# W_o's product in whole fp32 instead of three products of rounded parts, and new orders of work on all engines

## The reference

```
xn  = layernorm(x)                                       # plain
x2  = layernorm(xn) * ln_w + ln_b                        # the attention's own
q, k, v = x2 W_q + b_q, x2 W_k + b_k, x2 W_v + b_v       # 16 heads of 64
P   = softmax(q k^T / 8, causal)                         # 256 x 256 for each head
z   = P v                                                # per head
attn = sum over heads of z W_o + b_o                     # back to 128 features
Wq  = clip(round(W / (mean|W| + 1e-5)), -1, 1)           # ternary, for W1 and W2
ffn = relu(xn Wq1^T + b1) Wq2^T + b2                     # 512 hidden
out = x + attn + ffn
```

## Time and profile before

| | |
|---|---|
| runs | 227.25, 227.69, 225.07 us |
| the profiled execution | 226.65 us, its span 224.9 us |
| PE busy | 212.5 us (95%), 3670 matmul records |
| DVE busy | 202.1 us (90%) |
| ACT busy | 195.7 us (87%) |
| POOL busy | 182.5 us (81%) |
| granted TensorE clock | full (1.00) in all stretches |

### The profile page before, as it was taken

How to read it: one execution, slowest core, us unless ns; L and a number is a source line. 1 busy time by engine, 2 the same in 40 slices (tenths; PEclk the granted TensorE clock), 3 DMA queues, 4 the chain that set the end, 5 groups by cost and what they waited for, 6 DMA issues and landing times.

```text
span 224.9 us, 9676 instructions
## 1 busy us (share of the span) xinstructions
PE 212.5 (95%) x3670; PEld 187.4 (83%) x3670; DVE 202.1 (90%) x776; ACT 195.7 (87%) x733; POOL 182.5 (81%) x363
## 2 busy tenths in 40 slices
PE   7999799999999999989998999999997999999885
PEld 5666489779997999879997999989986998799674
DVE  3298999999999998999999999999999998899921
ACT  1799999989999889997999889997999799997740
POOL 5569999999979995899959995999959995955630
PEclk9999999999999999999999999999999999999999
DMA  5890538503875658624855658634865748638700
GB/s 149 273 281 6 124 72 219 155 0 59 236 190 136 138 109 208 146 54 111 184 153 136 127 112 217 137 67 111 188 154 126 142 102 207 166 66 210 167 11 23
DMA packets 24030, 30.79 MB, mean 137 GB/s; under 512 B 2608, under 2 KB 23088, under 8 KB 23984
## 3 DMA queue, kind: packets, MB, share of 16 engines
q1 hardware_dynamic: 23840, 30.16, 56.0%
q10 hardware_dynamic: 144, 0.02, 0.0%
HBM read 4.73 MB, written 1.05 MB: 26 GB/s over the span
## 4 chain that ended last, share of the span: by engine, by line
PE 38%; DVE 23%; DMA 11%; ACT 10%; POOL 8%; SPq 4%; issue 3%; POOLq 0%; DVEq 0%
DMA pT<-blocks 11%; DVE s_ps L604 9%; PE m_ps L863 6%; PE s_ps L823 6%; DVE blocks L617 6%; SPq L352 4%; ACT prob L492 3%; PE m_ps L941 3%; ACT prob L494 2%; PE m_ps L788 2%; PE s_ps L734 2%; DVE neg_max L604 2%; PE m_ps L790 2%; PE m_ps L789 2%; DVE zT_lo L623 2%
## 5 line engine op out<-in xcount | busy, mean ns | idle before, releaser
L492 ACT ACTIVATE prob<-s_ps,neg_max 128x256 f32<-128x256 f32 x128 | 65.4, 511 | 2.6 <-DVE neg_max L604 2.3
L315 POOL TENSOR_SCALAR prob<-prob,inv_sum 128x128 f32<-128x128 f32 x126 | 47.1, 374 | 22.1 <-DVE inv_sum L611 21.9
L604 DVE CUSTOM_DVE_ANT_0 s_ps<-s_ps,causal 128x256 f32<-128x256 f32 x128 | 55.8, 436 | 6.8 <-PE s_ps L823 6.5
L316 POOL TENSOR_SCALAR prob<-prob,inv_sum 128x256 f32<-128x256 f32 x126 | 61.3, 486 | 0.0
L617 DVE STREAM_TRANSPOSE blocks<-prob 128x768 f32<-128x768 f32 x62 | 58.8, 960 | 0.7 <-POOL prob L316 0.6
L863 PE MATMUL m_ps<-pT,v 64*64 64x64 f32 (+2 forms) x1536 | 50.0, 257 | 5.9 <-DMA pT<-blocks 3.5
L863 PEld LDWEIGHTS m_ps<-pT,v 64*64 64x64 f32 x1536 | 42.8, 133 | 12.1 <-issue 5.8
L494 ACT ACTIVATE prob<-s_ps,neg_max 128x128 f32<-128x128 f32 x128 | 51.7, 404 | 0.0
L823 PE MATMUL s_ps<-qk 64*64 64x128 f32 (+2 forms) x1280 | 49.7, 275 | 0.8 <-ACT prob L494 0.6
L823 PEld LDWEIGHTS s_ps<-qk 64*64 64x64 f32 x1280 | 42.1, 133 | 5.6 <-issue 3.3
L604 DVE CUSTOM_DVE_ANT_0 s_ps<-s_ps,causal_first 128x128 f32<-128x128 f32 x128 | 42.4, 331 | 0.0
(11 more groups left out here) (120 smaller groups left out, 492.1 us busy)
## 6 DMA issues: line engine op xcount, KB each, us to landing
pT<-blocks SPq DMA_DIRECT2D x124, 192.0 KB, 3.6
xT_cur<-in_xT SPq DMA_DIRECT2D x8, 128.0 KB, 4.6
outT<-out_sb SPq DMA_DIRECT2D x8, 128.0 KB, 4.1
x_all<-in_x SPq DMA_DIRECT2D x1, 768.0 KB, 8.9
wv_raw<-in_w_v SPq DMA_DIRECT2D x2, 256.0 KB, 5.9
wo<-in_w_o SPq DMA_DIRECT2D x1, 512.0 KB, 7.0
x_all<-in_x SPq DMA_DIRECT2D x2, 128.0 KB, 4.1
wq_raw<-in_w_q SPq DMA_DIRECT2D x2, 128.0 KB, 2.4
```

The lines of the kernel that those rows point to most:

```text
L315: op(first, first, inv_sum[:, j, 2 + h:3 + h], 0.0, ALU.mult, ALU.add)
L316: last = op(later, later, inv_sum[:, j, h:h + 1], 0.0, ALU.mult, ALU.add)
L492: nc.scalar.activation(later, s_ps[:, pair % 2, h, 0:S].rearrange("p (g j k) -> p g j k", g=TILES, j=QT), ACT.Exp, bias=neg_max[:, j, h:h ...
L604: last = nc.vector.tensor_tensor_reduce(out=sc, in0=sc, in1=mask, scale=-SCALE, scalar=-MASKED, op0=ALU.add, op1=ALU.min, accum_out=neg_ma ...
```

## The change: W_o and z stay whole, and the orders are new

W_o is kept as it comes from memory and z as one fp32 tile `zT`; each triple of float32r matmuls is now a single whole fp32 matmul. The two splitting steps of W_o and DVE's four `z` steps per batch are gone, with the tiles and semaphores that served them; where PE waited for DVE (`z_lo`) it now waits for ACT (`z_done`). P v itself (line 863) is as it was. All orders are written anew.

```diff
-PE_PLAN = ("s0 x0-:1 y0-:2 s1 z0- pr4:0 pr5:3 x1-:1 y1-:2 s2 z1- v0:0 pr6:3 x2-:2 y2-:1 s3 z2- s4 pr7:3 v1:0 "
-           "x3-:2 y3-:1 s5 z3- s6 v2:3 v3:0 xh+:2 oa-:1 f0:0 f1:2 s7 pr0+:0 xn+:3 pr1+:2 ob- pr2+:0 pr3+:3")
+PE_PLAN = ("pr5:3 x1-:1 y1-:2 s2 z1- s3 pr6:0 v0:3 x2-:1 y2-:2 s4 z2- pr7:3 x3-:1 v1:0 y3-:2 s5 z3- s6 v2:3 v3:2 "
+           "xh+:0 oa-:1 f0:0 f1:2 xn+:3 s7 pr0+:0 pr1+:2 ob- pr2+:3 pr3+:0 x0:2 s0+ y0:1 s1+ z0 pr4+:0")
...
-ACT_PLAN = ("e13- e14- pr0 xn e15- pr1 pr2 pr3 e0 z0- e1 e2 pr4 pr5 z1- e3 e4 e5 pr6 z2- e6 e7 e8 e9 pr7 z3- e10 "
-            "xh+ e11 e12 f0 f1")
+ACT_PLAN = ("e1 z0- e2 e3 pr4 pr5 z1- e4 e5 pr6 e6 z2- e7 e8 e9 pr7 z3- e10 xh+ e11 e12 e13 f0 xn+ f1 pr0+ pr1+ "
+            "e14 e15 pr2+ pr3+ e0+")
...
-DVE_PLAN = ("ln+ m2 z0- m3 i0 t7- m4 m5 z1- t0 i1 v0 m6 m7 z2- m8 m9 t1 i2 v1 m10 m11 i3 z3- v2 m12 i4 v3 xh+ t2 "
-            "t3 i5 m13 m14 m15 i6 t4 t5 xn+ t6 o- i7 m0+ m1+")
+DVE_PLAN = ("m2 m3 ln+ t7- i0 i1 m4 m5 t0 m6 v0 m7 t1 m8 i2 i3 m9 v1 m10 m11 i4 v2 m12 v3 xh+ m13 t2 t3 i5 xn+ i6 "
+            "t4 t5 m14 m15 t6 o- i7 m0+ m1+")
...
-POOL_PLAN = ("p1 ln+ p2 p3 xl+ p4 p5 p6 h0 p7 p0+ h1")
+POOL_PLAN = ("h0- h1- p0 p1 ln+ p2 p3 p4 xl+ p5 p6 p7")
...
-SP_PLAN = ("d3- d0 d1 d2 st-")
+SP_PLAN = ("d0 d1 d2 d3 st-")
...
-                nc.scalar.activation(zT_hi[:, 2 * duo:2 * duo + 2, :], heads_banks(duo, b), ACT.Copy).then_inc(z_hi, 1)
+                nc.scalar.activation(zT[:, 2 * duo:2 * duo + 2, :], heads_banks(duo, b), ACT.Copy).then_inc(z_done, 1)
...
-            def low_heads(b, duo):
-                wait(dve, z_hi, PAIRS // 2 * b + duo + 1)
-                both = slice(2 * duo, 2 * duo + 2)
-                nc.vector.tensor_tensor(zT_lo[:, both, :], heads_banks(duo, b), zT_hi[:, both, :].bitcast(F32),
-                                        ALU.subtract).then_inc(z_lo, 1)
...
                 for p in range(PAIRS // 2):
-                    nc.tensor.matmul(dst, wo_lo[:, p, :], zT_hi[:, p, :], start=False, stop=False)
-                    nc.tensor.matmul(dst, wo_hi[:, p, :], zT_lo[:, p, :], start=False, stop=False)
-                    nc.tensor.matmul(dst, wo_hi[:, p, :], zT_hi[:, p, :], start=False, stop=False)
+                    nc.tensor.matmul(dst, wo[:, p, :], zT[:, p, :], start=False, stop=False)
...
                     if p % 2 == 0:
-                        wait(pe, z_lo, DUOS * b + p // 2 + 1)
-                    nc.tensor.matmul(dst, wo_lo[:, p, :], zT_hi[:, p, :], start=False, stop=False)
-                    nc.tensor.matmul(dst, wo_hi[:, p, :], zT_lo[:, p, :], start=False, stop=False)
-                    last = nc.tensor.matmul(dst, wo_hi[:, p, :], zT_hi[:, p, :], start=False, stop=(p == PAIRS - 1))
+                        wait(pe, z_done, DUOS * b + p // 2 + 1)
+                    last = nc.tensor.matmul(dst, wo[:, p, :], zT[:, p, :], start=False, stop=(p == PAIRS - 1))
```

More of the change, by code:

```diff
@@ L58 @@
-ACT_HEAD = ("wh0 wh1 pr0 wh2 xn pr1 wh3 e0 e1 pr2 aa e2 pr3 e3 pr4 pr5 e4 e5 pr6 pr7 f0 e6 e7 xh+ e8 e9 xn+ f1 "
-            "e10 e11 pr0+ e12 e13 e14 e15 pr1+ oh z0 pr2+ e0+ wh4 e1+ pr3+ pr4+ z1 e2+ pr5+ e3+ e4+ e5+ z2 e6+ "
-            "wh5 e7+ pr6+ z3 e8+ e9+ xh++ pr7+ e10+ e11+ e12+ f0+ f1+")
-ACT_PLAN = ("e13- e14- pr0 xn e15- pr1 pr2 pr3 e0 z0- e1 e2 pr4 pr5 z1- e3 e4 e5 pr6 z2- e6 e7 e8 e9 pr7 z3- e10 "
-            "xh+ e11 e12 f0 f1")
-ACT_TAIL = ("e13- pr0 xn e14- pr1 e15- pr2 pr3 e0 e1 pr4 z0- e2 e3 z1- e4 e5 z2- pr5 e6 e7 pr6 e8 e9 pr7 z3- e10 "
-            "e11 e12 e13 z0 e14 e15 f0 z1 w6 w7 f1 z2 z3")
@@ L75 @@
-POOL_PLAN = ("p1 ln+ p2 p3 xl+ p4 p5 p6 h0 p7 p0+ h1")
-POOL_TAIL = ("p1 p2 p3 p4 p5 p6 h0 h1")
-SP_HEAD = ("d0 d1 d2 d3 d0+ d1+ d2+ st")
-SP_PLAN = ("d3- d0 d1 d2 st-")
-SP_TAIL = ("d3- d0 d1 d2 st- st")
+PE_HEAD = ("xb:1 pr0:3 pr1:1 xn:0 s0 pr2:3 v0:0 v1:2 s1 s2 v2:2 pr3:1 ta:0 pr4:3 s3 pr5:2 pr6:3 s4 v3:2 pr7:0 s5 "
[3 rows of a table added]
+PE_PLAN = ("pr5:3 x1-:1 y1-:2 s2 z1- s3 pr6:0 v0:3 x2-:1 y2-:2 s4 z2- pr7:3 x3-:1 v1:0 y3-:2 s5 z3- s6 v2:3 v3:2 "
+           "xh+:0 oa-:1 f0:0 f1:2 xn+:3 s7 pr0+:0 pr1+:2 ob- pr2+:3 pr3+:0 x0:2 s0+ y0:1 s1+ z0 pr4+:0")
@@ new lines @@
+PE_TAIL = ("s2 x1-:1 y1-:2 pr5:3 z1- s3 v0:0 pr6:2 pr7:1 v1:0 s4 x2-:2 y2-:3 s5 x3-:1 y3-:0 z2- z3- s6 v2:2 "
+           "oa-:3 x0:0 f0:2 y0:1 s7 ob- z0 x1:2 y1:3 f1:0 tw6:1 z1 v3:0 tn3:2 tw7:3 x2:0 y2:1 x3:3 y3:2 z2 z3 "
+           "oa:0 ob oc")
+ACT_HEAD = ("wh0 wh1 pr0 wh2 xn pr1 wh3 e0 e1 pr2 aa e2 e3 pr3 wh4 pr4 e4 e5 pr5 e6 e7 pr6 e8 e9 xh+ wh5 pr7 e10 "
+            "e11 f0 e12 pr0+ e13 pr1+ e14 e15 z0 e0+ pr2+ xn+ f1 e1+ pr3+ pr4+ pr5+ e2+ e3+ z1 e4+ e5+ e6+ pr6+ "
+            "e7+ z2 e8+ e9+ pr7+ z3 e10+ e11+ xh++ e12+ e13+ f0+ xn++ f1+ e14+ e15+ pr0++ pr1++ pr2++ pr3++ e0++")
@@ new lines @@
+ACT_PLAN = ("e1 z0- e2 e3 pr4 pr5 z1- e4 e5 pr6 e6 z2- e7 e8 e9 pr7 z3- e10 xh+ e11 e12 e13 f0 xn+ f1 pr0+ pr1+ "
+            "e14 e15 pr2+ pr3+ e0+")
+ACT_TAIL = ("e1 z0- e2 e3 e4 pr4 z1- pr5 e5 e6 pr6 e7 pr7 e8 e9 z2- e10 e11 e12 z3- e13 f0 e14 e15 z0 f1 w6 z1 w7 "
+            "z2 z3")
+DVE_HEAD = ("lz nh xb xn m0 m1 ln+ v0 i0 v1 m2 wl0 m3 m4 wl1 m5 v2 i1 th m6 te0 i2 m7 m8 t0 m9 t1 m10 i3 i4 m11 "
[3 rows of a table added]
+DVE_PLAN = ("m2 m3 ln+ t7- i0 i1 m4 m5 t0 m6 v0 m7 t1 m8 i2 i3 m9 v1 m10 m11 i4 v2 m12 v3 xh+ m13 t2 t3 i5 xn+ i6 "
+            "t4 t5 m14 m15 t6 o- i7 m0+ m1+")
@@ new lines @@
+DVE_TAIL = ("m2 m3 i0 t7- m4 t0 m5 i1 m6 v0 m7 t1 i2 v1 m8 m9 i3 m10 m11 t2 t3 i4 m12 i5 v2 m13 t4 t5 i6 m14 m15 "
+            "o- i7 q7 v3 n3 o")
+POOL_HEAD = ("hs np wl2 p0 ln+ p1 p2 wl3 p3 xl+ p4 wl4 p5 p6 p7 wl5 h0 p0+ p1+ h1 ln++ p2+ p3+ xl++ p4+ p5+ p6+ "
+             "p7+")
+POOL_PLAN = ("h0- h1- p0 p1 ln+ p2 p3 p4 xl+ p5 p6 p7")
+POOL_TAIL = ("h0- p0 h1- p1 p2 p3 p4 p5 p6 h0 h1")
+SP_HEAD = ("d0 d1 d2 d3 d0+ d1+ d2+ d3+ st")
+SP_PLAN = ("d0 d1 d2 d3 st-")
+SP_TAIL = ("d0 d1 d2 st- st")
@@ L176, in attention_ffn_kernel @@
         hT_lo = sb("hT_lo", [P, FC, S], F32R)
-        zT_hi = sb("zT_hi", [P, PAIRS, S], F32R)
-        zT_lo = sb("zT_lo", [P, PAIRS, S], F32R)
+        zT = sb("zT", [P, PAIRS, S])
         xT_cur = sb("xT_cur", [D, 2, S])
@@ L222, in attention_ffn_kernel @@
         exp_done = sem("exp_done")
-        z_hi = sem("z_hi")
         f_done = sem("f_done")
@@ L242, in attention_ffn_kernel @@
         last_narrow = sem("last_narrow")
-        z_lo = sem("z_lo")
+        z_done = sem("z_done")
         v_done = sem("v_done")
@@ L461, in _ @@
                     hidden(b, index)
-                elif kind == "wl":
+                else:
                     low_part(nc.gpsimd.tensor_tensor, pool, index)
[L464 to L467, removed]
         @block.scalar
@@ L748, in wait_taken @@
                 elif kind in "xy":
-                    wait(pe, z_lo, PAIRS // 2 * b + index + 1)
+                    wait(pe, z_done, PAIRS // 2 * b + index + 1)
                 elif kind == "tw":
@@ L936, in first_output @@
                     pe.wait_ge(tern_ready, 2)
-                    pe.wait_ge(wo_lo_done, 1)
+                    pe.wait_ge(wo_in, 16)
                 wait(pe, h_ready, 2 * b + 2)
@@ L941, in first_output @@
                         nc.tensor.matmul(dst, w2T[:, c, :], hid[:, c, :], start=(hid is hT_hi and c == 0), stop=False)
-                wait(pe, z_lo, PAIRS // 2 * b + 2)
+                wait(pe, z_done, PAIRS // 2 * b + 2)
                 for p in range(PAIRS // 2):
-                    nc.tensor.matmul(dst, wo_lo[:, p, :], zT_hi[:, p, :], start=False, stop=False)
-                    nc.tensor.matmul(dst, wo_hi[:, p, :], zT_lo[:, p, :], start=False, stop=False)
-                    nc.tensor.matmul(dst, wo_hi[:, p, :], zT_hi[:, p, :], start=False, stop=False)
+                    nc.tensor.matmul(dst, wo[:, p, :], zT[:, p, :], start=False, stop=False)
             def last_output(b, duos):
```

15 lines of the change are left out of this document (removed), and 12 rows, old and new, of tables (DVE_HEAD, PE_HEAD).

## The result

The changed kernel takes **229.07 us** (median of 3 runs, 228.49 to 229.45) where the kernel before took 227.25 (225.07 to 227.69). The ratio is 1.012, with a 95% interval of 1.007 to 1.017. That is slower by less than 2%, and above the range of the prediction (220.8 to 228.2). The profiled execution took 228.49 us with a span of 226.7; before's had 226.65 and 224.9.

The account below looks back on a forecast made before the run. Bound: a loop through VectorE's run, transpose, DMAs and PE. Periods -0.8, opening -1.4, end -0.9 make -3.1, say -3.2, from 226.65 to 223.5; the median stands 0.6 higher, so 224.0 us, range 220.8 to 228.2.

Parts of the forecast that it names:

- the sum for a period: Middle periods: 12.4 - 0.55 + 12.8 + 0.66 = 25.3, floor 24.5, taken as 25.05; five periods -0.8 us.
- PE's own work in the loop: From s0 to y3-, PE itself needs 11.0 us, so about 1.4 of its 12.4 us are waits.
- the prediction's loop: Middle: s0, VectorE's run, t7, the DMAs, y3 (12.4 us), then PE without pause to the next s0 (12.8 us).
- PE gets more work: W_o's products in oa and ob: whole fp32 0.43 us against 0.35 for three matmuls, +0.66 us a batch.
- VectorE: Loses four subtractions a batch, 684 ns each; in the middle only one is on the path, landing 0.55 us earlier.
- ScalarE's copy: ScalarE copies z as before, 617 ns, the same bytes: no effect on the time.
- Rival 3: ScalarE becomes the bound, s4 waiting for exponentials by 0.2 us; if they come later, 226 us; chance 0.16.
- Rival 2: Before y3- the landing comes no earlier and PE's extra work is paid in full: about 229 us; chance 0.12.
- Rival 1: VectorE was the bound, its 2.7 us a batch come free, period 24.5 to 24.6: 221.5 us; chance 0.22.
- Opening: Before oa of batch 0, ScalarE, POOL and VectorE all shrink, by the least 1.18 us: -1.4 us.
- End: Last stretch: two subtractions off the chain -1.1, o- behind the transpose -0.4, PE's work +0.66: -0.9 us.

Follow-up runs that it names:

- e1: Changed kernel's whole fp32 W_o product without the splitting steps, but with the orders of the kernel before: 228.44 us, ratio 1.009 to before.
- e6: Changed kernel with the copy z1 moved from ScalarE to VectorE, behind m5: 227.26 us, ratio 1.004 to before.
- e7: Kernel before with the transpose t7- moved ahead of the statistics ln+ in VectorE's order: 226.06 us, ratio 0.998 to before.
- e9: Kernel before's orders without VectorE's z steps, W_o as three float32r matmuls of one rounded product: 223.06 us, ratio 0.983 to before.
- e8: Kernel before with W_o's product whole fp32, splits and VectorE's subtractions kept and waited for: 231.36 us, ratio 1.022 to before.
- e4: Changed kernel with a spare 128x256 ScalarE copy per batch, inside the run of exponentials from s0 to s4: 230.88 us, ratio 1.021 to before.
- e5: Changed kernel with the same spare ScalarE copy placed outside the stretch from s0 to s4: 228.60 us, ratio 1.008 to before.

## Why the prediction was wrong

**The step that failed** is in the sum for a period, in two terms that belong together. The first is the size of PE's own work in the loop: "Sum ... = 11.0 us. So about 1.4 us of PE's 12.4 are waits", and from it "From below the loop cannot beat PE's own work, 11.0 + 12.8 + 0.66 = 24.5". e1 shows that stretch at 11.6, of which 0.2 is a wait for ScalarE, so 11.4. The waits were then 1.0 a period, not 1.4. The terms left out are small ones that come often: 0.10 in the first of the three pieces, 0.13 in the second, 0.15 in the third.

The second term is ScalarE, put at "nothing", and for `s4` at 0.2 us "inside a stretch that waits for the DMA anyway". In the changed kernel each of the five periods is 12.20 us from `s0` to `y3-` and 13.6 from there to the next `s0`; the prediction's loop had 12.4 - 0.55 = 11.85 and 12.8 + 0.66 = 13.46. In the 12.20 stand the 0.61 us that `s4` waits for `e5`, and no wait for the DMA is left to cover them. Without them the period would be 25.15, a tenth from the 25.05 forecast, and e6, which takes one copy out of ScalarE's run, has 25.3. Five times 0.61 is 3.1 of the 3.2 us that the five periods missed. That 25.05 lies so close to PE's own pace is luck: it was set two thirds of the way from a floor of 24.5 that was too low to a loop that no longer held.

Before's orders would not have saved the forecast. In e1 the five periods take 128.18 us, 1.7 more than before instead of 0.8 less, by waits for ScalarE and for the landing; the new orders have 0.6 more.

**The loop before** was read correctly as far as the landing went, but the two periods read were not all of them. In the fourth, `y3-` came 147.60 - 135.94 = 11.66 us after `s0` without a wait, and PE waited for ScalarE instead:

```profile
135.94 0.78 PE L823 MATMUL s_ps<-qk 64*64 64x256 f32 x20
...
147.60 0.78 PE L863 MATMUL m_ps<-pT,v 64*64 64x256 f32 x20
...
149.71 0.79 PE L823 MATMUL s_ps<-qk 64*64 64x256 f32 x20 [0.23 <-ACT prob L494]
```

So both things that failed could be seen in the trace of before: a stretch of 11.66 bounds PE's own work from above, and ScalarE's exponentials stood behind the landing. e7 adds a third: subtractions that free the P v banks stood ready as well. The prediction put their removal at nothing, since it would "only turn into a longer wait at `y3-`". In truth relief of VectorE was worth 1.3 to 1.7% over the whole kernel. In the middle e9, which has the relief without the price, is 0.34 us a period under before, not 0.55; the rest is in the opening (0.2 us), the sixth period (0.5) and the end (0.8).

**PE gets more work, +0.66 a batch: right** in size. W_o's four products with the matmul behind them take 1.84 us less that matmul's 0.12, so 1.72. `oa` and `f0` together take 3.22 against 2.91 before, `ob` and `pr2` 2.43 against 2.12: +0.62. That holds for the periods of before from which the 0.118 a float32r matmul was read. In others the twelve take 1.36 us instead of 1.41, at the same granted clock of 1.00, and `oa` with `f0` takes 2.82 and `ob` with `pr2` 2.04: +0.77. The mean lies at 0.7. This term made the kernel slower: by the ratios to before, 5.0 us (e8) and 5.8 us (e1 against e9) over the same kernel with three matmuls. The Trainium skill (FP8 and Floating Point Precision, TensorE Precision Notes) says that true FP32 is four passes. By that a product would be 4 x 0.118 = 0.47 us, an estimate. The trace has 0.43, somewhat less, and the order of size agrees.

**VectorE: right** in size, 21.59 of 25 against the 21.7 named. **ScalarE's copy: right**, 636 ns against 617:

```profile
L494 ACT ACTIVATE zT<-m_ps 128x512 f32<-128x512 f32 x32 | 20.3, 636 | 2.5 <-PE m_ps L842 2.0
```

But "nothing" was wrong for where it stands, as said above. Two copies and six pairs of exponentials lie in a row before `s4`, and there each tenth counts (e4, e6).

**Rival 3 (ScalarE, `s4`) is the mechanism of the new orders' part.** It was given 0.2 us, "inside a stretch that waits for the DMA anyway". It is 0.6. Counted from the end of `s0`, as there, ScalarE begins after 0.86 us (0.6 was allowed), its run takes 7.39 and the step to PE 0.14 (7.3 for both), so `s4` may start at 8.4 and not 7.9; PE would be there at 7.8 (7.7). Two tenths too little at two places made a wait three times as long. And the cover was gone: no wait for the DMA was left in these periods. **Rival 2's** number, 229, was hit by another cause: the landing did come early enough. Its own terms, 3.3 + 1.3 - 1.4 on the 226.65 of the profiled execution, add to 229.9 and not to 229. **Rival 1** did not come: VectorE has slack now and the period did not fall. Only e9, its relief without PE's price, reached 223.06, with 24.7 to 24.8 us in three of five periods.

**Opening: -0.4 instead of -1.4.** I took all three engines to be full there and the least of the savings to pass through. Before's chain did run through POOL's split of W_o:

```profile
36.26 2.35 POOL wo_lo L466
```

It is gone, but other chains stood close behind. After, it runs through exponentials and the first landing:

```profile
33.76 0.49 ACT zT L494
34.25 0.45 ACT prob L482 x2
...
36.52 0.89 DVE blocks L604
...
41.58 5.17 DMA pT<-blocks
46.88 0.76 PE m_ps L842 x13
```

e1, with before's orders, has its first `oa` at 51.02, 0.33 earlier than before, and its chain from 35 to 51 us is almost PE alone. So it is not the new orders that lost the gain: less than half a us behind the old chain lay PE's own.

**End: -0.1 instead of -0.9,** which is two parts: the sixth period pays (+0.6), and the stretch behind it gains 0.8. Both come with the new orders: e1, which has the same product with before's, takes 24.00 for the sixth period and 23.43 behind it, where before has 24.13 and 22.93. So relief and price together come to -0.1 and +0.5 there, and the new orders cost 0.8 in the sixth period and give back 1.3 at the end. In the change the chain, which had VectorE's subtractions and a landing, is almost PE alone:

```profile
199.23 0.69 PE s_ps L802 x14
...
201.42 1.78 PE m_ps L842 x61
...
218.67 0.61 ACT zT L494
...
219.32 1.18 PE m_ps L920 x8
220.49 1.73 PE m_ps L923 x8
222.22 1.74 PE m_ps L930 x8
```

What stays open: which small PE terms make up the missing 0.4 us was read from start distances and not varied alone. Why float32r matmuls have two paces in before, and always the faster one in e9's middle, no run shows. Of e9's two longer periods the one of 25.13 has a wait of 0.83 us for the landing; the one of 25.40 has 0.60 us of idle time inside a P v block, for which the trace names no cause, as in e5. And the change was never run beside e1 on one chip, so their distance rests on ratios to before.

## What to carry to other kernels

When work moves from a helper engine to the tensor engine, sum the tensor engine's own time for a whole period from start distances, with every return from small tiles to the full array, before calling the rest of the period waits; look through all periods for the one that waits least, which bounds that sum. The relief is worth at most those waits, and here most of the price was paid beside it. A place where several waits stand behind each other (here the landing, the freed banks and ScalarE's exponentials) moves only as far as the next of them. When a step is moved forward in an order, add up the other engine's run to the item it needs, from the start of what triggers it: a spare copy in that run, and the same copy outside it, tell at once whether it is on the path.
